# A decoder layer on one core: the shift row of a sequence filled by one transfer instead of two

## The reference

```python
x = x + attn(layernorm(x), Wq, bq, Wk, bk, Wv, bv, Wo, bo)            # causal, with a slope per head
x = x + xattn(layernorm(x), ctx, ctx, Wq, bq, Wk, bk, Wv, bv, Wo, bo)  # 120 context tokens
x = x + tanh(layernorm(x) @ weight @ aux_weight1 @ aux_weight2 + bias)

# inside attn:
scores = einsum('bhqd,bhkd->bhqk', q, k) * scale + alibi_bias_causal
out = einsum('bhqk,bhkd->bhqd', softmax(scores), v)
```

## Time and profile before

| what | value |
|---|---|
| median of 3 runs | 2377.55 us (2377.23 to 2383.47) |
| the profiled execution | 2373.22 us |
| its span | 2371.5 us |
| PE busy | 2229.0 us, 94% |
| PEld busy | 1848.5 us, 78% |
| DVE, ACT, POOL busy | 72%, 60%, 30% |
| mean granted PE clock | 0.984 of full speed |

### The profile page before, as it was taken

How to read it: one execution, slowest core, us unless ns; L and a number is a source line. 1 busy time by engine, 2 the same in 40 slices (tenths; PEclk the granted TensorE clock), 3 DMA queues, 4 the chain that set the end, 5 groups by cost and what they waited for, 6 DMA issues and landing times.

```text
span 2371.5 us, 67224 instructions
## 1 busy us (share of the span) xinstructions
PE 2229.0 (94%) x22072; PEld 1848.5 (78%) x22072; DVE 1708.8 (72%) x3710; ACT 1416.2 (60%) x3066; POOL 719.2 (30%) x1372
## 2 busy tenths in 40 slices
PE   4799999999999999999999999999999999999985
PEld 3588887887887887887888888788788788788764
DVE  4477777777777777777877877777777777777762
ACT  2466666666666666666666666666666666666651
POOL 3132333333233233233233233323323323323321
PEclk9899999999999999999999999999999999999995
DMA  6533433433443443443343344344344344344320
GB/s 134 124 95 106 109 107 95 118 106 98 115 107 89 109 120 85 113 111 96 103 116 98 104 107 108 95 116 107 98 113 110 86 109 120 88 111 111 98 73 23
DMA packets 167370, 244.83 MB, mean 103 GB/s; under 512 B 22176, under 2 KB 90512, under 8 KB 164248
## 3 DMA queue, kind: packets, MB, share of 16 engines
q1 hardware_dynamic: 165660, 244.22, 39.0%
q10 hardware_dynamic: 1664, 0.01, 0.1%
HBM read 53.13 MB, written 33.56 MB: 37 GB/s over the span
## 4 chain that ended last, share of the span: by engine, by line
PE 75%; DVE 8%; issue 5%; POOL 4%; DMA 3%; ACT 2%; SPq 2%; DVEq 0%; POOLq 0%; ACTq 0%
PE ps_misc L555 14%; PE ps_misc L541 14%; PE ps_score L630 7%; PE ps_max L612 5%; PE ps_score L639 5%; PE ps_score L629 4%; PE ps_attend L654 4%; PE ps_misc L684 4%; DVE neg_max_s L975 4%; PE ps_max L600 3%; PE ps_misc L525 3%; PE ps_misc L699 3%; PE ps_attend L673 2%; DMA q_stack<-neg_max_t_s 2%; PE ps_misc L566 2%
## 5 line engine op out<-in xcount | busy, mean ns | idle before, releaser
L813 ACT ACTIVATE probs<-ps_score 128x384 f32<-128x384 f32 x1024 | 476.2, 495 | 145.7 <-PE ps_score L630 142.7
L975 DVE TENSOR_REDUCE neg_max_s<-ps_max 128x2 f32<-128x512 f32 (+1 forms) x768 | 479.2, 679 | 5.7 <-PE ps_max L594 4.5
L820 ACT ACTIVATE xprobs<-ps_score 120x512 f32<-120x512 f32 x512 | 292.5, 597 | 251.6 <-PE ps_score L639 213.5
L1113 POOL TENSOR_SCALAR ve_LN<-mv_LN 128x2 f32<-128x2 f32 x192 | 37.0, 193 | 1112.7 <-DVE mv_LN L997 1092.7
L983 DVE TENSOR_REDUCE neg_max_x<-ps_max 128x4 f32<-128x480 f32 x512 | 316.6, 650 | 21.3 <-PE ps_max L612 9.6
L630 PE MATMUL ps_score<-q_stack,k_stack 128*128 128x256 f32 x1024 | 321.6, 335 | 0.0
L629 PE MATMUL ps_score<-q_stack,k_stack 128*128 128x128 f32 x1024 | 292.6, 286 | 17.7 <-DMA q_stack<-neg_max_t_s 12.3
L629 PEld LDWEIGHTS ps_score<-q_stack,k_stack 128*128 128x128 f32 x1024 | 194.7, 190 | 62.9 <-DMA q_stack<-neg_max_t_s 29.3
L1141 POOL TENSOR_TENSOR res<-res,chain_n 128x512 f32<-128x512 f32 x64 | 81.6, 1275 | 410.2 <-ACT chain_n L858 410.2
L639 PE MATMUL ps_score<-xq_stack,xk_stack 128*120 128x256 f32 x1024 | 201.6, 309 | 4.4 <-DMA xq_stack<-neg_max_t_x 3.5
L600 PE MATMUL ps_max<-k_stack,q_stack 127*128 127x256 bf16 x1024 | 194.8, 281 | 4.5 <-DVE neg_max_s L975 0.7
(11 more groups left out here) (147 smaller groups left out, 5379.2 us busy)
## 6 DMA issues: line engine op xcount, KB each, us to landing
k_stack<-k_nat SPq DMA_DIRECT2D x192, 256.0 KB, 3.8
q_stack<-q_nat SPq DMA_DIRECT2D x192, 256.0 KB, 3.7
xq_stack<-q_nat SPq DMA_DIRECT2D x192, 256.0 KB, 3.7
xk_stack<-scr_xk SPq DMA_DIRECT2D x192, 128.0 KB, 2.7
x_in<-in_x SPq DMA_DIRECT2D x64, 256.0 KB, 2.7
scr_xk<-k_nat SPq DMA_DIRECT2D x32, 512.0 KB, 3.0
out_y<-res SPq DMA_DIRECT2D x64, 256.0 KB, 2.2
ctx_in<-in_ctx SPq DMA_DIRECT2D x32, 240.0 KB, 3.0
```

The costliest lines, as they stand in the source:

```text
L813: act.activation(probs[:, h % 8, :], bank_of("SCORE", i, b, h)[:, P:4 * P], ACT.Exp)\
L820: act.activation(xprobs[0:C, at:at + 2, :], blocks(bank_of("XSCORE", i, b, u))[0:C], ACT.Exp).then_inc(sem("xprobs_ready"), 1)
L975: dve.tensor_reduce(o, ins, AX.X, ALU.max, negate=True).then_inc(sem("max_taken"), 1)
```

## The change

`neg_max` is laid out as queries by head by block instead of queries by block by head. Its transpose then has row 2 h + a for head h and block a. Read row after row, that is the order of the shift row, so one transfer of 16 KB from 32 partitions fills the whole row, seen as one contiguous run of 4096 numbers. The waits on its semaphore go from 32 to 16 for a sequence. The reductions write every second number of a partition of `neg_max` instead of adjacent ones. The same is done for the cross attention.

```diff
-        neg_max = {n: sb(f"neg_max_{n}", [P, NB, H]) for n in ("s", "x")}
+        neg_max = {n: sb(f"neg_max_{n}", [P, H, NB]) for n in ("s", "x")}
...
-                    for qb in range(NB):
-                        sp.dma_start(dst_of(b)[SHIFT:SHIFT + 1, :, qb * P:(qb + 1) * P].bitcast(F32),
-                                     neg_max_t[which][qb * H:(qb + 1) * H, :])\
-                            .then_inc(sem(f"{which}_shift_stacked"), 16)
+                    sp.dma_start(dst_of(b)[SHIFT:SHIFT + 1, :, :].rearrange("r h t -> r (h t)").bitcast(F32),
+                                 neg_max_t[which][:, :]).then_inc(sem(f"{which}_shift_stacked"), 16)
...
-                    pe.transpose(bk[0:NB * H, 0:P], neg_max[which][:, :, :].rearrange("p a h -> p (a h)"),
+                    pe.transpose(bk[0:NB * H, 0:P], neg_max[which][:, :, :].rearrange("p h a -> p (h a)"),
...
-                    wait(pe, "s_shift_stacked", 32, i, b, 32)
+                    wait(pe, "s_shift_stacked", 16, i, b, 16)
...
-                    wait(pe, "x_shift_stacked", 32, i, b, 32)
+                    wait(pe, "x_shift_stacked", 16, i, b, 16)
...
-                    wait(act, stacked, 32, i, b)
+                    wait(act, stacked, 16, i, b)
...
-                    ins, o = blocks(bk, 4), neg_max["s"][:, 0, 4 * g:4 * g + 4]
+                    ins, o = blocks(bk, 4), neg_max["s"][:, 4 * g:4 * g + 4, 0]
...
-                    ins, o = blocks(bk), neg_max["s"][:, 1, h:h + 2]
+                    ins, o = blocks(bk), neg_max["s"][:, h:h + 2, 1]
...
-                dve.tensor_reduce(neg_max["x"][:, qb, 4 * g:4 * g + 4], bk, AX.X, ALU.max,
+                dve.tensor_reduce(neg_max["x"][:, 4 * g:4 * g + 4, qb], bk, AX.X, ALU.max,
```

## The result

The changed kernel takes 2367.94 us (median of 6 runs, 2365.83 to 2369.39), the kernel before in the same comparison 2377.57 us (6 runs, 2376.39 to 2383.47). The ratio on record is 0.9955 with a 95% interval of 0.9942 to 0.9967: 0.45% faster. It is not the quotient of the two medians (0.9960), between which lie 9.6 us. The profiled executions are 2373.22 and 2365.83 us long, with spans of 2371.5 and 2364.1 us.

The account below looks back on a forecast made before the run. In the loop only PE's wait for the self shift row was taken to matter, about 0.42 us a step. Gains of 4.8 us in the loop and 1.7 at beginning and end, 6.5 off 2377.55, gave 2371.0 us; range 2366 to 2377.

Parts of the forecast that it names:

- One transfer less, landing: Shift row: one issue less on SP, data landing after 1.85 us at +2.21, 0.58 us sooner.
- The rival of one engine taking the row in turn: Shift row's 32 pieces pass one DMA engine, landing in 2.9 us; slower, 2407 us; chance 0.07.
- Head 0 and the room: Self scores: head 0 starts 0.45 us sooner; landing may come 0.4 us after +2.21 before anything is lost.
- What is late next: Loop step: line 684 stays at +3.59 waiting for DVE; `XQ` starts 0.15 and 0.08 us sooner.
- What takes part of that back: Behind `XQ`: `LN1_T` waits for POOL and `XOUT_T` follows it, to +8.11; 0.09 and 0.08 us kept.
- the rival "more": Loop: `XOUT_T` hangs on the bank of `XQ`, so all 0.15 and 0.08 us arrive; 8.1 us, 2369.4 us; chance 0.20.
- the three signs of being wrong: In the trace after: line 684 moves, `XOUT_T` moves by more than `LN1_T`, or the landing takes over 2.3 us.
- Beginning and end: Outside the loop: three issues of about 0.58 us fall off the chain, 1.7 us gained.
- The reductions: Reductions writing `neg_max` with gaps cost 0; bounds 0 and 1.3 us.
- SP's other transfers: `XK_STACK` and later transfers on SP start up to 0.58 us sooner but were covered; costed at nothing.
- "hidden": Loop: POOL holds `LN1_T` where it is, only the 1.7 us outside the loop remain; 2375.9 us; chance 0.15.
- "the issue all on the path": Loop: the saved issue counts in full, 62 x 0.58 us = 36 us; 2341.6 us; chance 0.03.

Follow-up runs that it names:

- probes: Changed kernel plus single transfers of 4 to 16 KB at the end, each waited for before the next; only landings read, 1.6 to 2.1 us.
- pad_ahead: Changed kernel with one small transfer into an unused tile issued ahead of the self shift transfer; 2396.26 us, ratio 1.0084 to the kernel before.
- halves: Changed kernel with PE transposing the first half of each layer norm's output while POOL makes the second; 2352.15 us, ratio 0.9898 to the kernel before.
- halves_two_transfers: Kernel before, two transfers per shift row kept, with layer norms handed from POOL to PE in halves; 2372.17 us, ratio 0.9981.
- pool_late_bias: Changed kernel with POOL's addition of the bias to the residual moved behind `LN1`; 2367.35 us, ratio 0.9965 to the kernel before.
- layout_only: Changed kernel's new layout, but each shift row filled by two transfers of 8 heads; 2376.76 us, ratio 1.0001 to the kernel before.
- pad_behind: Changed kernel with one small transfer into an unused tile issued behind the self shift transfer; 2365.81 us, ratio 0.9951 to the kernel before.

## Why the prediction came out as it did

**One transfer less, landing.** The issue went as forecast. The landing was mis-sized: 1.85 us taken, 2.1 measured. So head 0 came 0.30 us sooner and not the 0.45 forecast; it still starts with the landing. I had divided the packets' time by 16 engines, but these bytes all go into one partition, and the probes put 0.3 us between 8 and 16 KB there and none when 16 KB go to 16 partitions. The Trainium skill (DMA: Bandwidth & Descriptors, Specifications; SBUF — State Buffer, Door 1: The DMA port swizzle) has a partition reached through one port of 32 B at 850 MHz; an estimate from that is 0.3 us for 8 KB more. The probes agree with it (1.8 to 2.1 us). The rival of one engine taking the row in turn is out: 2.1 us and not 2.9.

**Head 0 and the room.** The wait that counted went, since the landing, some 0.04 us ahead of head 0's +2.53, is still earlier than where it begins to count. The room was given as 0.4 us from +2.21, that is up to +2.61. Measured with `pad_ahead` it is 0.21 us from head 0's +2.53, so a landing up to about +2.70 is free. So the longer landing used up more than half of the room, and nothing of the gain was lost by it.

**What is late next.** Right in kind: line 682 waits for DVE, `XQ` follows it by 0.84 us, and counted from line 682 `XQ` is sooner by about the 0.15 and 0.08 us predicted (0.99 and 0.92 us behind it before, 0.84 and 0.84 after: 1223.81 - 1222.97, and 1258.11 - 1257.27 in the other kind). `halves` shows that this chain binds, and `halves_two_transfers` that before the change head 0's path bound `XQ`.

**What takes part of that back: the step that failed.** The forecast let `XOUT_T` follow `LN1_T`, which POOL would hold, and so kept back part of `XQ`'s gain; it put 0.17 us on a pair, and 0.26 was measured. Its evidence was a distance from `LN1_T` to `XOUT_T` of 2.06 and 2.07 us. But its own rows hold a distance that is as constant, the one from `XQ` to `XOUT_T`: 3.62 us (1226.05 to 1229.67), 3.64 and 3.61 ahead of the loop. The runs tell the two apart. `XOUT_T` takes the bank of `XQ`, which DVE's line 958 (956 after) gives back. The two kinds of step before:

```profile
1228.68 0.88 DVE L958 SCALAR_TENSOR_TENSOR q_nat<-ps_misc,bias_xq,q_nat 128x256 fp32r<-128x256 f32 x2 [2.21 <-ACT q_nat L806]
...
1263.17 0.88 DVE L958 SCALAR_TENSOR_TENSOR q_nat<-ps_misc,bias_xq,q_nat 128x256 fp32r<-128x256 f32 x2 [2.22 <-ACT q_nat L806]
```

And after:

```profile
1226.43 0.88 DVE L956 SCALAR_TENSOR_TENSOR q_nat<-ps_misc,bias_xq,q_nat 128x256 fp32r<-128x256 f32 x2 [2.05 <-ACT q_nat L804]
...
1257.27 0.42 PEld L682 LDWEIGHTS ps_misc<-ident,heads_t 128*128 128x128 f32 x4 [0.59 <-DVE chain_t L947]
...
1258.11 0.31 PEld L539 LDWEIGHTS ps_misc<-chain_t,w_xq_hi 128*128 128x128 f32 x2
...
1260.82 0.88 DVE L956 SCALAR_TENSOR_TENSOR q_nat<-ps_misc,bias_xq,q_nat 128x256 fp32r<-128x256 f32 x2 [2.14 <-ACT q_nat L804]
...
1261.74 0.42 PEld L697 LDWEIGHTS ps_misc<-ident,chain_n 128*128 128x128 f32 x4
```

`XOUT_T` starts 0.11 and 0.05 us behind DVE's end before (1229.67 and 1264.10) and 0.11 and 0.04 us after (1227.42 and 1261.74). In the loops of all traced versions it starts 3.60 to 3.67 us behind `XQ`, but for the one disturbed step of `halves_two_transfers`, while `LN1_T` starts anywhere from 1.44 to 1.58 us behind `XQ`. `pool_late_bias` moves `LN1_T` by 0.12 us and `XOUT_T` by nothing. So `XQ`'s gain arrives whole. The profile names DVE as the releaser in one kind of step only the earlier trace rows; in the other it names none, and the constant distance is the evidence.

The +8.11 that was forecast came true all the same, and this hid the error. It was read from a step ahead of the loop in which line 684 stands at +3.66 (203.61 - 199.95), and put beside a forecast that kept line 684 at +3.59. In the loop after, line 682 stands at +3.66 too, because the point counted from, ACT's copy, moved: POOL's line 1125 began 0.44 us after the copy (1219.75 and 1219.31 above), where the same work of the kernel before had begun 0.36 us after its copy at 1221.47:

```profile
1221.83 1.10 POOL L1127 TENSOR_SCALAR chain_n<-res,rstd_LN,nmr_LN 128x256 f32<-128x256 f32 x2 [0.21 <-POOL nmr_LN L1122]
```

Counted from the `XOUT_T` of the step before, POOL's start is 28.09 us in both kernels and the copy 27.74 us before and 27.66 after (medians). So it is the copy that came sooner, and in this kind of step everything on POOL's chain, line 682 among it, reads 0.07 or 0.08 us later. Counted from that line instead, `XOUT_T` went from 4.61 us behind it to 4.45 (1222.97 to 1227.42): the full 0.16 us. In the other kind of step it went from 4.56 to 1261.74 - 1257.27 = 4.47. Together this is 0.25 us, the pair's gain. It is the rival "more" that held, with its 0.15 + 0.08 us a pair and 8.1 us in all. It had been given a chance of 0.20; the forecast with the failed step had 0.52.

Of the three signs of being wrong two came: line 684 moved by 0.07 us, and `XOUT_T` moved by more (8.20 to 8.11) than the load of `LN1_T` (6.03 to 6.07) or its product (6.13 to 6.08). The landing stayed under 2.3 us.

**Beginning and end.** 1.7 us were forecast from three issues; the profiles show 1.6 us in the first five steps and 1.7 at the end. Yet `layout_only`, whose median is that of the kernel before, shows 180.05 us for the first five steps and 163.8 us behind the 62nd copy. So most of what the two profiles differ by there can be scatter between executions, and the part of the change in it is not resolved. 7.2 us of loop are shown. The ratio's interval is 7.8 to 13.8 us (0.9967 to 0.9942), so beginning and end probably give something too; how much is open.

**The reductions.** Costed at nothing, and nothing is seen (`layout_only` 1.0001, 0.9992 to 1.0010). The two shapes after, against the earlier trace rows:

```profile
L973 DVE TENSOR_REDUCE neg_max_s<-ps_max 128x2 f32<-128x512 f32 x512 | 326.2, 678 | 1.2 <-PE ps_max L598 1.1
...
L973 DVE TENSOR_REDUCE neg_max_s<-ps_max 128x4 f32<-128x512 f32 x256 | 173.9, 679 | 4.0 <-PE ps_max L592 4.0
```

**SP's other transfers.** Covered, as `pad_behind` shows from the other side: one more issue there moves nothing.

**The whole.** The mechanism held up to `XQ` and failed behind it, where the gain passed by `LN1_T`. That the time still lies in the range is in part luck and no proof of the forecast: the range was drawn to hold the rivals "more" and "hidden" too. The loop's term was 4.8 us and measured 7.2; 2.4 us of the 3.1 us by which the forecast missed the median are this one term. The rivals "hidden", "the issue all on the path" and "one engine" are excluded by the pair's 0.26 us (they ask for 0, 1.16 and -0.94).

## What to carry to other kernels

When one wait goes, write the instruction behind it as the later of two bounds, here `XQ` = max(head 0 + 1.76, line 684 + 0.85): the first edit gains only up to the second bound, and the second edit only together with the first. The single transfer is worth 0.26 us a pair by itself and 0.66 once the layer norm is split (70.37 to 69.71), while the split alone is worth nothing in the loop. Before a constant distance is taken for a dependence, look whether another instruction stands at a distance as constant: two of them are told apart only by a run in which they move against each other. And measure gains from a point on the chain that stays put, not from one that the change itself moves.

## What the runs showed of the hardware

A transfer that fills one partition lands 0.2 us later for 8 KB than for 4 KB and 0.3 us later again for 16 KB (1.6, 1.8, 2.1 us), while 16 KB over 16 partitions, neighbours or 8 apart, take 1.7 us. An issue on SP took 0.50 to 0.58 us in the median, whatever the bytes (502 ns from 4 to 16 KB into one partition, 519 ns for the shift row, 572 ns in the loop). So two transfers of half a row land the second half at 0.58 + 1.8 us, one transfer the whole at 2.1: the gain is the issue less 0.3 us. By an estimate from these figures it would be gone at a row about twice as long, if both go on growing as here; that was not run.
